# Reordering the drain of a linear-attention stage and splitting the routing tables of a mixture-of-experts stage

## What is computed

```
x = x + cross_attention(layernorm(x), ctx)          # 64 batches, 257 context rows each
x = x + linear_attention(layernorm(x))              # 16 heads of 64, elu+1 features, cumulative over 32 tokens, gated
x = x + mixture_of_experts(layernorm(x))            # 8 experts, top 2, silu(x w1) * (x w3) times w2
```

## Time and profile before

| | |
|---|---|
| median of three runs | 871.98 us (870.95 to 873.74) |
| the profiled execution | 874.67 us, its span 872.8 us |
| TensorE busy | 800.7 us (92%) |
| VectorE, ScalarE, GpSimd busy | 642.8, 556.3, 252.9 us |
| mean granted TensorE clock | 0.945 |

### The profile page before, as it was taken

One profiled execution on the slowest core, in us unless ns is written; L12 is line 12 of the kernel. 1 busy time (PEld: TensorE's weight loads), 2 busy tenths in 40 slices (PEclk: granted clock), 3 DMA queues, 4 the chain that ended last, 5 costly groups with the idle time before them and its releaser, 6 DMA issues.

```text
span 872.8 us, 23910 instructions
## 1 busy us (share of the span) xinstructions
PE 800.7 (92%) x9166; PEld 693.0 (79%) x9166; DVE 642.8 (74%) x1044; ACT 556.3 (64%) x858; POOL 252.9 (29%) x149
## 2 busy tenths in 40 slices
PE   5899989999999999999753799999999999999994
PEld 4466578899989999897643688898888889889883
DVE  4344443757747576464766699999999999999991
ACT  2344547645646556373211689999999999999981
POOL 2344400000000000000000155555554655555551
PEclk8799999999999999998665799999999999999997
DMA  9999910000000000007262244554554455455442
GB/s 344 404 409 415 419 72 2 2 15 3 26 28 3 27 3 26 18 12 304 122 228 111 81 134 121 148 146 127 139 153 129 129 151 141 120 153 143 125 136 45
DMA packets 31769, 115.90 MB, mean 133 GB/s; under 512 B 4465, under 2 KB 11570, under 8 KB 26578
## 3 DMA queue, kind: packets, MB, share of 16 engines
q1 hardware_dynamic: 22834, 100.17, 31.9%
q0 software_dynamic: 8864, 14.69, 7.9%
HBM read 105.27 MB, written 9.57 MB: 132 GB/s over the span
## 4 chain that ended last, share of the span: by engine, by line
PE 83%; DVE 6%; DMA 4%; issue 2%; ACT 2%; SPq 1%; POOLq 0%; POOL 0%; DVEq 0%; ACTq 0%
PE ps L453 21%; PE ps L455 20%; PE ps L454 20%; PE ps L795 4%; PE ps L641 3%; PE ps L620 2%; PE ps L552 2%; PE ps L629 2%; PE ps L499 2%; PE ps L533 1%; DMA stage<-in_w_a 1%; PE ps L511 1%; DMA ctx_t<-in_ctxT 1%; PE ps L758 1%; PE ps L691 1%
## 5 line engine op out<-in xcount | busy, mean ns | idle before, releaser
L1433 DVE TENSOR_TENSOR w_lo<-w,w_hi 128x1024 fp32r<-128x1024 f32 x156 | 186.2, 1213 | 1.4 <-issue 1.4
L1000 ACT ACTIVATE w_hi<-w 128x1024 fp32r x156 | 161.0, 1057 | 10.1 <-DMA w<-in_w 9.0
L439 POOL DMA_INDIRECT out_x<-y_sb,slot_row x39 | 130.3, 3341 | 112.7 <-ACT y_sb L1032 112.7
L453 PE MATMUL ps<-w_hi,xh 128*128 128x512 f32 x312 | 127.0, 407 | 1.3 <-DVE xl L1519 1.3
L455 PE MATMUL ps<-w_hi,xl 128*128 128x512 f32 x312 | 123.0, 394 | 0.0
L454 PE MATMUL ps<-w_lo,xh 128*128 128x512 f32 x312 | 122.8, 393 | 0.0
L453 PE MATMUL ps<-xT_hi,wa_hi 128*128 128x256 f32 x384 | 111.7, 291 | 0.6 <-DVE kT L1215 0.6
L454 PE MATMUL ps<-xT_lo,wa_hi 128*128 128x256 f32 x384 | 107.5, 280 | 0.8 <-issue 0.8
L455 PE MATMUL ps<-xT_hi,wa_lo 128*128 128x256 f32 x384 | 107.4, 280 | 0.0
L428 POOL DMA_INDIRECT xs_sb<-xn_d,slot_row x39 | 68.0, 1743 | 105.5 <-PE ps L758 77.7
L1011 ACT ACTIVATE w_hi<-w_sb 128x1024 fp32r<-128x1024 f32 x78 | 82.7, 1061 | 24.6 <-PE ps L455 11.8
(11 more groups left out here) (200 smaller groups left out, 1716.3 us busy)
## 6 DMA issues: line engine op xcount, KB each, us to landing
w_sb<-in_w SPq DMA_DIRECT2D x78, 512.0 KB, 4.3
ctx_t<-in_ctxT SPq DMA_DIRECT2D x16, 1028.0 KB, 9.5
ctx_n<-in_ctxN SPq DMA_DIRECT2D x16, 1024.0 KB
w<-in_w SPq DMA_DIRECT2D x8, 2048.0 KB, 14.2
stage<-in_w_a SPq DMA_DIRECT2D x16, 256.0 KB, 9.1
x_all<-in_x SPq DMA_DIRECT2D x4, 512.0 KB, 9.6
out_x<-x_all POOLq DMA_DIRECT2D x8, 256.0 KB, 3.4
xn_d<-xn POOLq DMA_DIRECT2D x8, 256.0 KB, 3.0
```

The lines of the kernel that those rows point to most:

```text
L439: pool.indirect_dma_start(out, bass.IndirectOffsetOnAxis(slot_row[:, t:t + 1], 0), y_sb[:, :], None, compute_op=ALU.add).then_inc(f_st, 16)
L453: pe.matmul(dst, l_hi, r_hi, start=first, stop=False)
L1000: act.activation(w_hi[:, c, :].rearrange("p (c n) -> p c n", c=DC), w13[:, bass.ds(e, 1), c % 2, :, c // 2 * 512:(c // 2 + 1) * 512].rearr ...
L1433: dve.tensor_tensor(w_lo[:, c, :].rearrange("p (c n) -> p c n", c=DC), w13[:, bass.ds(e, 1), c % 2, :, c // 2 * 512:(c // 2 + 1) * 512].re ...
```

## The change

- The queues at the end of the attention are in another order. In the last `astep` both score steps come directly behind the value projection, with the fourth gate projection between them, and ahead of the output projection of round 6, which moves into `drain`, on both sides of the denominators. The steps of `drain` are interleaved anew on TensorE, ScalarE and VectorE.
- `top_two(0)` covers 12 tiles and `top_two(1)` the last four; the ranks, places and one-hots are made once, for all 16 tiles, behind the last round. The softmax of the two scores moves ahead of `places`.
- The one-hots are made by two engines: four groups on VectorE as before and four on ScalarE as `Relu(1 - |i - inf|)`, five instructions each.
- `what` is split: `what_id` (40 columns) and `what_w` (80 columns). TensorE makes the 32 matmuls twice, first for the token numbers, then for the weights. `slot_row` follows the first pass, `slot_w` the second.
- Expert 0's weights load after six rounds' transposes and stores rather than eight, ahead of experts 2 and 3; experts 4 to 7 also wait for the last gate projection. The first down weights wait for the second pass.
- Buffers move to make this possible (the normalised tiles are in two places).

```diff
@@ SyncE
         load_expert(1)
         sp.wait_ge(a_v, 4 * NT // 2)
+        sp.wait_ge(a_gt, 4 * NT // 2)
         for e in range(E // 2, E):
             load_expert(e)
+        sp.wait_ge(g_tr, XN_T // 2)
+        sp.wait_ge(g_keep, 16 * XN_T // 2)
+        load_expert(0)
         sp.wait_ge(a_num, NT)
+        load_expert(2)
         sp.wait_ge(a_y, NT // 2)
-        for e in (2, 3):
-            load_expert(e)
-        sp.wait_ge(g_tr, NT // 2)
-        sp.wait_ge(g_keep, 16 * NT // 2)
-        load_expert(0)
+        load_expert(3)
...
         sp.wait_ge(r_done, 1)
+        sp.wait_ge(r_tab, 1)
         load_w2(0)
@@ TensorE
-            a_gates(r)
+            a_gates(r, range(4) if r < NR - 1 else range(3))
             for s in range(2):
                 if before:
                     a_nums(r - 1, s)
                 a_values(r, s)
+            if r == NR - 1:
+                a_scores(r, 0)
+                a_gates(r, range(3, 4))
+                a_scores(r, 1)
+                return
...
         def drain(r, u):
+            a_proj(r - 1, 1 - u, 0)
+            a_dens(r)
+            a_proj(r - 1, 1 - u, 1)
             g_trs(0)
             g_trs(1)
             g_logits(0)
+            a_nums(r, 0)
             g_trs(2)
-            a_dens(r)
-            for k in range(1, 4):
-                g_logits(k)
-                g_trs(k + 2)
+            g_logits(1)
+            g_trs(3)
+            g_logits(2)
+            a_nums(r, 1)
+            g_trs(4)
+            g_logits(3)
+            g_trs(5)
             g_logits(4)
-            for s in range(2):
-                a_nums(r, s)
+            a_proj(r, u, 0)
             g_logits(5)
+            a_proj(r, u, 1)
             g_trs(6)
             g_logits(6)
-            for s in range(2):
-                a_proj(r, u, s)
-            g_ranks(0)
             g_trs(7)
             g_logits(7)
+            ranks()
...
-                m = pe.matmul(ps[:, 6, 0:3 * TW], in_slot[:, n, :], what[:, n, :, :].rearrange("p k t -> p (k t)"),
+                m = pe.matmul(ps[:, 6, 0:TW], in_slot[:, n, :], what_id[:, n, :], start=n == 0, stop=n == TOP * NT - 1)
+        m.then_inc(r_rows, 1)
+        for q in range(TOP * NT // 4):
+            if q % 4 == 0:
+                pe.wait_ge(r_what, 2 * (q // 4 + 1))
+            for n in range(4 * q, 4 * q + 4):
+                m = pe.matmul(ps[:, 7, 0:2 * TW], in_slot[:, n, :], what_w[:, n, :, :].rearrange("p k t -> p (k t)"),
                               start=n == 0, stop=n == TOP * NT - 1)
         m.then_inc(r_tab, 1)
@@ ScalarE
         def drain(r, u):
-            for k in range(3):
+            den_ev(r)
+            for k in range(4):
                 g_xT_ev(k)
-            den_ev(r)
-            for k in range(3, 6):
-                g_xT_ev(k)
+            gated_hi(r, u, 0)
+            g_xT_ev(4)
             g_sqrt(r - 1)
-            gated_hi(r, u, 0)
+            g_xT_ev(5)
+            gated_hi(r, u, 1)
             g_xT_ev(6)
-            gated_hi(r, u, 1)
             g_sqrt(r)
             g_xT_ev(7)
+
+        def in_slots(qs):
+            for k, q in enumerate(qs):
+                wait(act, r_ain, k - 1)
+                for j in range(4):
+                    m = act.activation(apart[:, k % 2, j, :], con[:, C_I128:C_I128 + P], ACT.Abs, scale=-1.0,
+                                       bias=inf[:, 4 * q + j:4 * q + j + 1])
+                m.then_inc(r_apart, 1)
+                act.wait_ge(r_apart, k + 1)
+                act.activation(in_slot[:, 4 * q:4 * q + 4, :].rearrange("p n s -> p (n s)"),
+                               apart[:, k % 2, :, :].rearrange("p n s -> p (n s)"), ACT.Relu, scale=-1.0, bias=ones[:, 0:1]).then_inc(r_ain, 1)
@@ VectorE
+        def counts():
             for b in scan:
                 link(dve.memset(b[:, 0:8, :], 0.0))
             link(dve.tensor_copy(scan[0][:, 8:8 + LATE_T, :], both[:, 0:LATE_T, :]))
...
+        def drain(r, u):
+            masks(r)
+            g_lns(r - 2)
+            recip(r, 0)
+            recip(r, 1)
+            x2(r - 1)
+            norm_att(r, 0)
+            recip(r, 2)
+            recip(r, 3)
+            norm_att(r, 1)
+            gated(r, u, 0)
+            g_stats(r - 1)
+            gated(r, u, 1)
+            gated_lo(r, u, 0)
+            gated_lo(r, u, 1)
+            g_lns(r - 1)
+            top_two(0)
+            x2(r)
+            g_stats(r)
             g_lns(r)
-            places(0)
-            in_slots(range(0, 2 * LATE_T // 4))
+            counts()
```

More of the change, by code:

```diff
@@ L205, in build @@
     v_sb = place("v_sb", [P, 2, HF])
-    what = nc.alloc_sbuf_tensor_at("what", [P, NT * TOP, 3, TW], F32R, offset=at["low"])
+    what_id = nc.alloc_sbuf_tensor_at("what_id", [P, NT * TOP, TW], F32R, offset=at["low"])
+    what_w = nc.alloc_sbuf_tensor_at("what_w", [P, NT * TOP, 2, TW], F32R, offset=at["low"] + 4 * NT * TOP * TW)
+    gol_at = at["low"]
     gol = nc.alloc_sbuf_tensor_at("gol", [P, 2, FC, 2 * P], F32R, offset=at["low"])
@@ L222, in build @@
     rstd3 = place("rstd3", [P, 2])
+    sc_at = at["low"]
     sc = place("sc", [P, NT, E])
@@ L234, in build @@
     dv = place("dv", [P, NT])
+    spare = place("spare", [P, SLOT_TILES])
     assert at["low"] <= W13_AT, (at, W13_AT)
@@ L242, in build @@
     cmp = place("cmp", [P, E, MAXT])
[L243 to L246, removed]
+    cmp2 = nc.alloc_sbuf_tensor_at("cmp2", [P, SLOT_TILES, E], F32, offset=sc_at)
+    assert sc_at + 4 * SLOT_TILES * E <= pick_at
     prod = place("prod", [P, NT * TOP, E])
@@ L251, in build @@
     tef = place("tef", [P, SLOT_TILES])
-    spare = place("spare", [P, SLOT_TILES])
+    assert at["low"] <= cmp2_at + 4 * (2 * HF - NT * TOP * TW)
     at["low"] = experts_at
@@ L302, in build @@
         "part", "var", "sq", "rs", "ln", "tr", "xT", "mm", "sc", "max", "idx", "keep"))
-    r_step, r_d, r_e1, r_both, r_rank, r_what, r_in, r_tab, r_map, r_done = (
-        sem("r_" + n) for n in ("step", "d", "e1", "both", "rank", "what", "in", "tab", "map", "done"))
+    r_step, r_d, r_e1, r_both, r_rank, r_id, r_what, r_in, r_rows, r_tab, r_map, r_done, r_w = (
+        sem("r_" + n) for n in ("step", "d", "e1", "both", "rank", "id", "what", "in", "rows", "tab", "map", "done", "w"))
+    g_keep2, r_inf, r_apart, r_ain = sem("g_keep2"), sem("r_inf"), sem("r_apart"), sem("r_in_act")
     o_init = sem("o_init")
@@ L595, in a_qks, with a_gates @@
                 across(n % 4, (n % 2) * HF + (n // 2) * 2 * P).then_inc(a_qk, 1)
-        def a_gates(r):
-            for n in range(4):
+        def a_gates(r, ns=range(4)):
+            for n in ns:
                 wait(pe, a_qku, 8 * r + n + 5)
+                if r == NR - 1 and n == 3:
+                    wait(pe, a_vu, 4 * r + 4)
                 across(n, 3 * HF + n * 2 * P).then_inc(a_gt, 1)
@@ L604, in a_values @@
                 n = 2 * s + j
-                wait(pe, a_gtu, 4 * r + n + 1)
+                wait(pe, a_qku if r == NR - 1 and n == 3 else a_gtu, 8 * r + 8 if r == NR - 1 and n == 3 else 4 * r + n + 1)
                 f = 2 * HF + j * 512
@@ L962, in astep @@
                 values(r, s)
+            if r == NR - 1:
+                gates(r, u, range(3, 4))
             a_hi_ev(r + 1)
@@ L1376, in in_slots @@
                                   ALU.is_equal).then_inc(r_in, 1)
-        def drain(r, u):
-            masks(r)
-            g_stats(r - 1)
-            recip(r, 0)
-            recip(r, 1)
-            norm_att(r, 0)
-            g_lns(r - 1)
-            recip(r, 2)
-            recip(r, 3)
-            norm_att(r, 1)
-            for s in range(2):
-                gated(r, u, s)
-                gated_lo(r, u, s)
-            top_two(0)
-            wait(dve, a_y, NR)
+        def counts():
             for b in scan:
```

150 lines of the change are left out of this document (82 added, 68 removed).

## The result

| | before | changed |
|---|---|---|
| median of 4 runs each (us) | 872.51 (870.95 to 873.74) | 863.71 (863.29 to 866.22) |
| profiled execution / span (us) | 874.67 / 872.8 | 863.29 / 860.7 |
| mean granted clock | 0.945 | 0.952 |

The ratio on record is 0.9877, with a 95% interval from 0.984 to 0.9914: 1.2% faster. (It is not the quotient of the two medians, which is 0.990.) The forecast of 860.0 is 3.7 us too low, and the time lies in the range. The unaltered changed kernel, measured again later in six runs, gave 0.991 (0.9879 to 0.9941). By the two ratios the gain is about 8 to 11 us, by the differences of the medians 8.8 and 6.4. The two profiled executions differ more, by 12.1 us of span.

A forecast was written before the change was run, and what follows sets the result against it. TensorE's waits between 400 and 484 us were taken as the bound. First expert matmul from 484.34 to 471.7 saves 12.6, counted as 12: 874.67 to 862.7 profiled, less 2.7 to the median, 860.0 us; range 850 to 866.

The forecast's parts named there:

- Part 1: Scores ahead of the projections: scores end at 399.7 us, denominators start at 402.6 instead of 411.3.
- I count at nothing here: TensorE's unexplained 1.60 us standstill in the second scores, left out of part 1; the sum keeps half of one.
- this first fall: The granted clock's fall at 408.6 us, after the standstill amid the scores; the new order was to remove it.
- Rival 3: Standstills in bursts of 128 small matmuls while expert loads fill the DMA engines: 4 us more, 865 us; chance 0.10.
- Part 2: The attention's tail: second numerators at 414.25 us, half clock from about 413, last addition at 443.0 instead of 456.2.
- rival 1: The clock holds through the drain: first expert matmul at 464.7, 19.6 us saved, 852.5 us; chance 0.25.
- Part 3: Routing: two table passes of 7.05 us each, the weights' pass and VectorE set the end, first expert matmul at 471.7.
- rival 4: ScalarE late with its one-hots, 1.28 us table loads twice a group, first pass waits 8.6 us: 868 us; chance 0.04.
- Rival 2: Table passes cost by columns, 2.4 and 4.7 us: 856 us with the clock down, 849 up; chance 0.08.
- Part 4: Expert loads: earlier load 0 saves nothing beyond keeping ScalarE's wait for weights off the path; up to 12 us if failing.
- Rivals 1, 5 and 6: 5: expert loop 0.4 us slower a tile, 876 us, chance 0.03. 6: round 7's projection stays last, 869, chance 0.05.

The follow-up runs named there:

- x12: The changed kernel run again, unaltered, on another chip than its first run; median 867.66 us, ratio to before 0.991.
- x1: Changed kernel with the loads of experts 4 to 7 also waiting for round 6's output projection; ratio to before 0.9906.
- x8: Changed kernel with the first tile's two low halves on VectorE ahead of `slot_w`, behind half the second pass; ratio to before 0.9875.
- x2: Changed kernel with the table made in one pass of 120 columns instead of two; ratio to before 0.9895.
- x10: x8 plus constant matmuls that nobody reads, ahead of the first pass, between the passes and ahead of the gathered tile's transposes; 857.26 us, ratio to before 0.9798.
- x4: Changed kernel with the expert loads in the order of the kernel before; ratio to before 0.9898.
- the nine drains: Drain times of the changed kernel, x1 to x4, x7, x8, x10 and x12, whose drain code is the same; 48.6 to 53.4 us, mean 51.2.
- x6: Changed kernel with 14 tiles in `top_two(0)` and two in `top_two(1)`, as before; 869.61 us, ratio to before 0.9934.
- x5: Changed kernel with the last step's old TensorE order, scores behind half projections of round 6; 867.93 us, ratio to before 0.9916.
- x3: Changed kernel with all eight groups of one-hots on VectorE, none on ScalarE; ratio to before 0.9918.
- x7: Changed kernel with six constant fp32 matmuls (twelve in the trace) that nobody reads, ahead of the table passes; ratio to before 0.9899.
- x11: x10 plus constant matmuls behind three of the drain's groups of gate scores; 855.66 us, ratio to before 0.978.

## Why the prediction was right, step by step

The sign, the place and the range were right, and the forecast of the median was 3.7 us low. Of that 0.6 is the profiled execution (862.7 forecast, 863.29 measured). The other 3.1 is the last step of the sum: 2.7 was taken off because the old profile lay that far above its median, and the changed kernel's profile lies 0.4 below its own. One execution's distance from its median is no property of the kernel that a change carries over. The 0.6 in turn lies outside the span: 2.6 us of the changed execution are around it, where 1.87 were assumed. The span itself was forecast at 860.8 and measured at 860.7, and that is luck, for three errors cancel: the values ended 0.85 us earlier than assumed, drain and routing together took 2.6 longer than their terms, of which the sum had kept 0.6, and the stretch behind them, which was held constant, was 1.2 shorter. x12, the same kernel, has a drain 2 us and a rest 2 us longer. In the changed kernel's rest the clock came back at 477.2, 3.8 us into the first tile, where before it took 6.2.

**Part 1: the mis-sized term.** The forecast had the denominators 6.9 us behind the values (395.7 to 402.6); they came 11.6 behind (394.85 to 406.46), 4.7 more. The standstill that "I count at nothing here" was 2.15 us, with 0.51 more in the gate projection; half a projection took 4.5 us in place of 2.9, since the clock fell at 402.1 and rose at 405.6. The prediction says that the new order removes this first fall; it didn't. The 0.6 us that the sum kept for a standstill was about a quarter of it. The denominators themselves ran at the full clock (1.88 us, forecast 1.7). Rival 3 named the effect and mistook the cause: x1 has it without the expert loads, and the wait ends 1.3 us behind a packet of instructions. (In the working behind this part the terms up to the second normalisation add to 413.0 and not 412.8, and the clock's return at 415.4 in the old kernel lies in the gate scores, not in the denominators, which had ended at 414.94.)

**Part 2.** The second numerators came 23.9 us behind the values (418.75), forecast 18.55 (414.25): 5.35 late, part 1's 4.7 and 0.65 more. The clock fell at 415.8, as chosen over rival 1 (forecast about 413). It came back at 429.4, in the first half of the last projection (4.4 us for the forecast 5.1) and ahead of the gate scores behind it (0.95 for 1.9), which gave 1.6 back. The last addition ended 50.3 us behind the values, forecast 47.3. So the order of waits held throughout, and of 4.7 us lost in part 1 three were left. The page "TensorE: Matmul & The Clock Gate" of the Trainium skill (Part 4: PE-mode transpose) says that a transpose doesn't count as TensorE activity the way a matmul does. The fall at 402.1 has score products, a gate projection and 2.15 us of idle time ahead of it and no transpose, so that rule alone doesn't explain it.

**Part 3.** Nearly all of it stood. A group on ScalarE took 1.26 for four Abs and 0.72 for the Relu with its gap, 1.93 us (forecast 2.1), and the last Relu ended at 456.40. No table load stands beside Abs or Relu, which is what "ScalarE: Activation LUTs" of the Trainium skill (Table sets: the hidden batching unit) says; rival 4 falls with these rows. `slot_row` came at 462.63 (forecast 460.8, with 2.2 us of lateness from the drain), `w_lo` at 470.69 took 2.36 us behind 1.07 us of register reading. From the end of the last addition to the first expert matmul it took 28.27 us, forecast 28.7. By x8 VectorE does set its end; by x2 the second pass costs 0.8 us more than the earlier gather gains.
Rival 2, the price by columns, falls by three widths. The page "TensorE: Matmul & The Clock Gate" of the Trainium skill (LDWEIGHTS) gives the loading of weights as about their columns over 1.2 in nanoseconds, by which 128 columns are estimated at 107; x10's first pass at full clock is 3.73 / 32 = 117 ns, so the trace agrees within a tenth, and at the lower clock it is 218 ns.

**Part 4.** No wait for weights came (ScalarE was released by `tile_e`), and by x4 none would have come in the old order either.

**Rivals 1, 5 and 6.** The clock didn't hold (0.67 over the stretch). The expert loop is no slower: the rest is 387.26 us for 388.46. The projection of round 7 does go ahead of the last ranks, and the drain is shorter.

**Where the gain came from.** Against the mean of the nine drains the old one, a single profile, is 9.3 us longer (60.5 and 51.2). The split into twelve and four tiles is 5.2 of it by its wait (x6; 5.7 by the whole drain), the order of scores and projections 2 to 3 (x5, inside the spread of 4.7). The third part is the one-hots, which stood ahead of the last addition. The old kernel's rows, of TensorE and of VectorE, show what they cost there:
```profile
449.76 1.87 PE L691 MATMUL ps<-gw,xT 128*128 128x8 f32 x8 [0.69 <-ACT xT L950]
...
454.31 0.16 DVE L1337 COPY sc<-ps 128x16 f32<-128x16 f32 x1
```
The last gate scores had ended at 451.63, and VectorE took them up behind its one-hots, 2.7 us later. The three add up to more than 9.3, within what single profiles can tell; no run put the one-hots back there, so their part is read and not tested. In the routing gains and costs cancel: the second engine is worth 2.4 us (x3), and from the last step of the places (`tilef`) to the first table matmul it is 2.1 us instead of 5.8, since the softmax, `tile_e` and the weights' part of `what` are no longer between them; against that stand the seven groups of one-hots moved into it (4.30 us in the earlier trace rows) and the second pass.

## What to carry to other kernels

Where two engines hand work to and fro at the end of a stage, look for what is queued behind a wait: the largest part of the gain was in splitting the one VectorE step that waited for TensorE's last scores, more than in issuing TensorE's own work earlier. Before moving bursts of small matmuls together, look at the instruction queue's packets: here 128 products took 1.3 us and the next 16 KB of instructions came 3.6 us or more behind the last. Price a stretch of light matmuls at either clock level, and if it is on the path, try dense products that nobody reads in the idle time ahead of it: here they and x8's reordering made the routing 7 us shorter, more than any part of the change. When one stage varies by 5 us between profiles and another by 0.03, judge each edit in its own stage before trusting the total.

## What the runs showed that I had not expected

- A product with 128x128 fp32r weights costs 0.22 us at 1.2 GHz, whether 40, 80 or 120 columns pass through it. At 2.4 GHz it is 0.117 with 40 columns and 0.127 with 80 (x10); 120 were not run at that level.
- TensorE stands still for 1.9 to 2.4 us ahead of the last three of 128 small score products, at the same instruction in all programs of the new order, with the DMA engines full or at 2%; in the old order it stands 1.60 to 1.96 us ahead of the last 51. The view of the waits names no releaser, but all 64 such idle times end 1.19 to 1.57 us behind a 16 KB packet of the instruction queue (see x1): it most likely waits for its own code.
- Constant matmuls in TensorE's idle time brought the clock back 3.1 us (x7) and 3.9 us (x10) after they began. In x7 it fell 3.0 us after they had ended; in x10, with one more between the passes, it stayed up through two light passes, and in x11, with the same, it fell as the second began. Why it held in one and not in the other isn't settled.
